# Entering the second attention: loads issued beside the last expert chunks, the norm in two halves, buffers laid out in another order

## The reference, cut to what matters

```python
# L1 ffn, per token: 8 routed experts of width 176 (2 chosen) and a shared one of 352
h1 = jnp.einsum('td,edh->eth', X, W1); h3 = jnp.einsum('td,edh->eth', X, W3)
y = jnp.einsum('eth,ehd->etd', jax.nn.silu(h1) * h3, W2)
out = jnp.einsum('etd,te->td', y, gate_full) + shared
x = x + out
# L2 attention on xn = layernorm(x): 16 query heads, 4 key/value heads, head width 128
q = rms_norm((xn @ wq), q_norm_w); k = rms_norm((xn @ wk), k_norm_w); v = xn @ wv
k_ctx = rms_norm(h_ctx_kv @ wk_ctx, k_norm_w); v_ctx = h_ctx_kv @ wv_ctx
q, k = q * cos + rotate_half(q) * sin, k * cos + rotate_half(k) * sin
probs = softmax(q @ concat([k_ctx, k]).T / sqrt(128) + causal)
x = x + (probs @ concat([v_ctx, v])).reshape(B, L, -1) @ wo
```

## Time and profile before

| | us |
|---|---|
| median of 3 runs | 2813.79 |
| lowest and highest | 2811.82, 2817.29 |
| the profiled execution, its own time | 2814.49 |
| its span | 2812.8 |
| PE busy | 2549.3 (91%) |
| DVE, ACT, POOL busy | 1729.9, 1483.5, 1358.1 |

### The profile page before, as it was taken

The page is one execution under the profiler, slowest core; times in us unless marked ns, Lnnn a source line. Parts: engine busy times, 40 slices in busy tenths (PEclk is TensorE's granted clock), DMA queues, the critical chain, the costliest instruction groups (busy, mean ns, idle before and its releaser), DMA issues. The chain is left out here.

```text
span 2812.8 us, 49623 instructions
## 1 busy us (share of the span) xinstructions
PE 2549.3 (91%) x16226; PEld 1756.5 (62%) x16226; DVE 1729.9 (62%) x3342; ACT 1483.5 (53%) x3294; POOL 1358.1 (48%) x913
## 2 busy tenths in 40 slices
PE   6889998949999999999999999999599699999997
PEld 4577776726777777777777777777355344444443
DVE  4355757547777777777777777777213655454445
ACT  2235444424555665555655555665113567676895
POOL 0025644414666765666756666767101365656400
PEclk9989999978999999999999999999699799999999
DMA  4212222120001000010000100002201000000100
GB/s 158 67 63 85 85 86 73 57 99 13 16 16 44 16 16 2 16 44 16 16 17 1 44 16 17 16 1 120 96 12 58 16 17 15 17 15 17 47 2 16
DMA packets 42454, 108.61 MB, mean 39 GB/s; under 512 B 5044, under 2 KB 26040, under 8 KB 37048
## 3 DMA queue, kind: packets, MB, share of 16 engines
q1 hardware_dynamic: 40424, 102.41, 10.9%
q0 software_dynamic: 768, 2.10, 0.2%
q10 hardware_dynamic: 1008, 0.79, 0.1%
HBM read 99.91 MB, written 4.98 MB: 37 GB/s over the span
## 5 line engine op out<-in xcount | busy, mean ns | idle before, releaser
L1141 POOL TENSOR_TENSOR xn<-xn,l_p 128x512 f32<-128x512 f32 (+1 forms) x400 | 631.4, 1578 | 176.0 <-ACT l_p L1181 155.4
L2120 ACT ACTIVATE l_p<-psum 128x1024 f32<-128x1024 f32 x416 | 394.4, 1022 | 132.6 <-PE psum L2240 132.3
L1266 DVE TENSOR_TENSOR l_plo<-l_p,l_phi 128x512 fp32r<-128x512 f32 (+1 forms) x464 | 398.9, 861 | 94.7 <-ACT l_p L1181 74.5
L1180 ACT ACTIVATE l_phi<-psum 128x512 fp32r<-128x512 f32 (+1 forms) x464 | 279.9, 603 | 272.8 <-PE psum L446 156.8
L1309 DVE TENSOR_REDUCE l_mx<-psum 128x1 f32<-128x512 f32 (+2 forms) x512 | 312.9, 618 | 77.0 <-PE psum L1470 72.8
L2094 POOL TENSOR_TENSOR l_rs<-l_ms,half_power 128x32 f32<-128x32 f32 x45 | 245.2, 5459 | 88.9 <-DVE l_ms L2145 88.9
L1181 ACT ACTIVATE l_p<-psum 128x512 f32<-128x512 f32 (+1 forms) x464 | 281.7, 607 | 0.0
L2240 PE MATMUL psum<-l_qT,l_kT 128*32 128x512 f16 x3328 | 256.4, 384 | 3.3 <-DVE l_qT L2001 2.9
L2250 PE MATMUL psum<-l_p,l_vs 128*32 128x256 f32 x3328 | 254.2, 380 | 0.3 <-ACT l_p L2120 0.3
L1470 PE MATMUL psum<-l_kThi,l_qThi 128*128 128x512 f32 (+2 forms) x512 | 212.4, 441 | 37.7 <-ACT l_kThi L1231 27.0
L1406 PE MATMUL psum<-l_m,l_ones 128*128 128x512 f32 (+1 forms) x464 | 227.3, 490 | 0.0
(11 more groups left out here) (375 smaller groups left out, 5228.4 us busy)
## 6 DMA issues: line engine op xcount, KB each, us to landing
w_stage<-in_L_w_dram SPq DMA_DIRECT2D x76, 384.0 KB, 3.1
l_w<-in_L_w_qkv_dram SPq DMA_DIRECT2D x16, 1024.0 KB, 4.9
l_ct<-in_ctx_tiles_dram SPq DMA_DIRECT2D x52, 128.0 KB, 2.1
c_T<-in_ctx_T_dram SPq DMA_DIRECT2D x4, 1601.0 KB
l_ctx<-in_ctx_T_dram SPq DMA_DIRECT2D x4, 1601.0 KB, 6.8
c_N<-in_ctx_dram SPq DMA_DIRECT2D x4, 1536.0 KB
s_wg<-in_L_gate_dram SPq DMA_DIRECT2D x4, 1024.0 KB, 11.5
s_wu<-in_L_up_dram SPq DMA_DIRECT2D x4, 1024.0 KB, 13.5
```

Source lines behind the costliest of these rows:

```text
L1141: g_.tensor_tensor(l2_acc[k][0:r, :], first[0:r, :], l2_p[c % 3][0:r, :], ALU.add)\
L1180: act.activation(l2_phi[c % 3][0:r, :], src, ACT.Exp).then_inc(l2_e, 1)
L1266: v.tensor_tensor(l2_plo[c % 3][0:r, :], l2_p[c % 3][0:r, :], l2_phi[c % 3][0:r, :].bitcast(F32), ALU.subtract)\
L2120: act.activation(l3_p[ring[c]][:, :], psum[:, (c % 2) * 2 * BANK:(c % 2 + 1) * 2 * BANK], ACT.Exp, scale=float(D3) ** -0.5).then_inc(l3_e, 1)
```

## The change

**The norm of the first half** (tiles 0 to 3) moves beside the last expert block: statistics on DVE and root on POOL at its chunk 5, rows on DVE at chunk 6, four transposes on PE and one copy on ACT at chunk 8 and again at chunk 10, through the bank `AUX`.

**The norm of the second half** (tiles 4 to 7) moves into the opening turn: statistics and root at step 12, rows at step 15, eight transposes and two copies at step 20. Only batches 2 and 3 read it.

**SP** issues `l2_ctx` and the first `l2_w` right behind the last expert weights, then waits for the first half's copies and issues `l2_xb`. After `x_upd` it issues the five small loads, then `l2_wo` on a semaphore of its own (`l2_oland`, for which PE waits before each output product), then the copies to `s_in`.

**POOL** clears the two `l2_m` and `l2_kraw` in place of DVE. ACT and DVE wait for all of POOL's constants (`later_consts` at 5) and five loads before the first copy and the rope products.

**Buffers** of this attention, of the next feed-forward stage (with a pad `s_pad`) and of the last attention are allocated in another order. No wait there is changed by it except the counts shown.

```diff
@@ expert stage @@
+        ATTENTION_NORMS = (NORMS[3][-1] + 1, NORMS[3][-1] + 2)
+        HALF_CP = (2 * len(BLOCKS) + 2, 2 * len(BLOCKS) + 4)
+        ATTENTION_STEP = {"stats": 5, "root": 5, "rows": 6, "turn0": 8, "turn1": 10}
+
+        def attention_rows(v, hf):
+            v.wait_ge(h_rs, ATTENTION_NORMS[hf] + 1)
+            for n in half_tiles(hf):
+                ins = v.tensor_scalar(xn[:, n, :], x[:, n, :], mv[:, n, 0:1], rstd[:, n:n + 1], ALU.subtract, ALU.mult)
+            ins.then_inc(h_xn, 1)
+
+        def attention_turn(pe, hf, c, at):
+            for n in half_tiles(hf):
+                mm = pe.transpose(bank(at, P, (n % HT) * P), xn[:, n, c * P:(c + 1) * P], ident[:, :])
+            mm.then_inc(h_T, 1)
+
+        def attention_copy(act, hf, c, at):
+            act.wait_ge(h_T, 2 * (len(BLOCKS) + hf) + c + 1)
+            act.activation(xT[:, c, half_cols(hf)], bank(at), ACT.Copy).then_inc(h_cp, 1)
...
                     if new is None:
+                        if i == ATTENTION_STEP["root"]:
+                            norm_root(g, ATTENTION_NORMS[0], 0)
                         continue
...
                     if new is None:
+                        for c in range(DC):
+                            if i == ATTENTION_STEP[f"turn{c}"]:
+                                attention_copy(act, 0, c, AUX)
                         continue
...
+                    elif i == ATTENTION_STEP["stats"]:
+                        v.wait_ge(x_upd, OUT_UPD[2])
+                        norm_stats(v, x_rows, 0)
+                    elif i == ATTENTION_STEP["rows"]:
+                        attention_rows(v, 0)
...
             else:
-                pe.wait_ge(x_upd, OUT_UPD[k - 1])
+                pe.wait_ge(h_cp, HALF_CP[0])
...
+                        if i == ATTENTION_STEP["turn0"]:
+                            pe.wait_ge(h_xn, len(BLOCKS) + 1)
+                            pe.wait_ge(x_upd, OUT_UPD[2])
+                            attention_turn(pe, 0, 0, AUX)
+                        if i == ATTENTION_STEP["turn1"]:
+                            pe.wait_ge(h_cp, 2 * len(BLOCKS) + 1)
+                            attention_turn(pe, 0, 1, AUX)
@@ second attention @@
+        SECOND_HALF_AT = (12, 12, 15, 20)
...
         def l2x_sync(sp):
-            sp.wait_ge(x_upd, X_AT[4])
-            rows = t["x"].rearrange("b s d -> (b s) d")
-            sp.dma_start(s_in[0:NTOK, :], rows).then_inc(s_pland, 16)
-            sp.dma_start(s_in[NTOK:TILES2 * P, :], rows[0:TILES2 * P - NTOK, :]).then_inc(s_pland, 16)
-            for dst, name in ((l2_cos, "rope_cos"), (l2_sin, "rope_sin"), (l2_kwc, "L2_kwc"), (l2_wo, "L2_wo")):
-                sp.dma_start(dst[...], t[name]).then_inc(l2_pland, 16)
...
-            sp.wait_ge(xT_cp, ln_l2x["cp_end"])
...
+            for b in range(B):
+                need(sp, l2_proj, b * (KH * NPROJ))
+                sp.dma_start(l2_ctx[:, :, :], t["ctx_T"][b]).then_inc(l2_cland, 16)
+                if b == 0:
+                    sp.dma_start(l2_w[:, :, :], t["L2_w_qkv"][0]).then_inc(l2_wland, 16)
+                sp.wait_ge(h_cp, HALF_CP[b // (B // 2)])
+                sp.dma_start(l2_xb[:, :, :], xT[:, :, b * S:(b + 1) * S]).then_inc(l2_cland, 16)
+                if b == 0:
+                    sp.wait_ge(x_upd, X_AT[4])
+                    for dst, name in ((l2_cos, "rope_cos"), (l2_sin, "rope_sin"), (l2_kwc, "L2_kwc")):
+                        sp.dma_start(dst[...], t[name]).then_inc(l2_pland, 16)
+                    for dst, name in ((l2_qw, "L2_qw"), (l2_kw, "L2_kw")):
+                        sp.dma_start(dst[:, :], t[name].to_broadcast([P, HD])).then_inc(l2_pland, 16)
+                    sp.dma_start(l2_wo[:, :, :], t["L2_wo"]).then_inc(l2_oland, 16)
...
+        def l2_clear(g):
+            g.wait_ge(x_upd, X_AT[4])
+            for s in range(2):
+                pool_steps.then(g, g.memset(l2_m[s][:, :, :].bitcast(F32), 0.0))
+            g.memset(l2_kraw[0][:, :, :], 0.0).then_inc(later_consts, 1)
...
+                    if g is None and c == SECOND_HALF_AT[1]:
+                        norm_root(g_, ATTENTION_NORMS[1], 1)
...
         def l2x_scalar(act):
-            norm_scalar(act, ln_l2x)
             act.preload_act_table(ACT.Exp)
-            act.wait_ge(l2_pland, 16 * 6)
+            act.wait_ge(l2_pland, 16 * 5)
+            act.wait_ge(later_consts, 5)
...
+                    if g is None and c == SECOND_HALF_AT[3]:
+                        for d in range(DC):
+                            attention_copy(act, 1, d, 3 + d)
...
         def l2x_vector(v):
             v.wait_ge(x_upd, X_AT[4])
-            dve_steps.then(v, v.memset(l2_kraw[0][:, :, :], 0.0))
...
-                dve_steps.then(v, v.memset(l2_m[s][:, :, :].bitcast(F32), 0.0))
-            v.wait_ge(l2_pland, 16 * 6)
+            v.wait_ge(later_consts, 5)
+            v.wait_ge(l2_pland, 16 * 5)
...
-            norm_vector(v, ln_l2x, x)
...
+                    if g is None and c == SECOND_HALF_AT[0]:
+                        norm_stats(v, x_rows, 1)
+                    if g is None and c == SECOND_HALF_AT[2]:
+                        attention_rows(v, 1)
...
         def l2x_tensor(pe):
-            norm_tensor(pe, ln_l2x)
...
                 if half == 0:
+                    pe.wait_ge(l2_oland, 16)
                     pe.wait_ge(l2_o, g * TB + (k + 1))
...
+                    if g is None and c == SECOND_HALF_AT[3]:
+                        pe.wait_ge(h_xn, len(BLOCKS) + 2)
+                        for d in range(DC):
+                            attention_turn(pe, 1, d, 3 + d)
...
+        sb("s_pad", [P, S_PAD], F32, top)
```

More of the change, by code:

```diff
@@ L39 @@
 TILES2 = NT + E2 - 1
+S_PAD = 2112
 QH, KH, HD = 16, 4, 128
@@ L981, in program @@
         TURNS = B * KH
-        l2_ctx = sb("l2_ctx", [P, DC, M], F32, l2)
-        l2_w = sb("l2_w", [P, DC, 4 * HD + REP * HD], F32, l2)
-        l2_xb = sb("l2_xb", [P, DC, S], F32, l2)
-        l2_kraw = [sb(f"l2_kraw{n}", [P, 4, HD], F32, l2) for n in range(2)]
-        l2_kn = [sb(f"l2_kn{n}", [P, 4, HD], F32, l2) for n in range(2)]
-        l2_ra = sb("l2_ra", [P, TB, HD], F32, l2)
-        l2_rb = sb("l2_rb", [P, TB, HD], F32, l2)
-        l2_q = sb("l2_q", [P, TB, REP, HD], F32, l2)
-        l2_qa = sb("l2_qa", [P, TB, REP, HD], F32, l2)
-        l2_qb = sb("l2_qb", [P, TB, REP, HD], F32, l2)
         def l2_slot(s):
@@ L1018, in program @@
         l2_ones = sb("l2_ones", [P, P], F32R, l2)
+        l2_wo = sb("l2_wo", [P, QH, D], F32, l2)
+        l2_ra = sb("l2_ra", [P, TB, HD], F32, l2)
+        l2_rb = sb("l2_rb", [P, TB, HD], F32, l2)
+        l2_q = sb("l2_q", [P, TB, REP, HD], F32, l2)
+        l2_qa = sb("l2_qa", [P, TB, REP, HD], F32, l2)
+        l2_qb = sb("l2_qb", [P, TB, REP, HD], F32, l2)
+        l2_xb = sb("l2_xb", [P, DC, S], F32, l2)
+        l2_ctx = sb("l2_ctx", [P, DC, M], F32, l2)
+        l2_w = sb("l2_w", [P, DC, 4 * HD + REP * HD], F32, l2)
+        l2_kraw = [sb(f"l2_kraw{n}", [P, 4, HD], F32, l2) for n in range(2)]
+        l2_kn = [sb(f"l2_kn{n}", [P, 4, HD], F32, l2) for n in range(2)]
+        l2_vhi, l2_vlo, l2_kThi, l2_kTlo, l2_qThi, l2_qTlo, l2_m = zip(l2_slot(0), slot1)
         l2.close()
+        l2_oland = sem("l2_oland")
         (l2_cland, l2_wland, l2_pland, l2_proj, l2_qc, l2_kvc, l2_vl, l2_ksqd, l2_kmsd, l2_krsd, l2_qmsd, l2_qrsd,
@@ new lines, in l2x_sync @@
+            for b in range(B):
[12 more added lines that the diff above has]
+                    sp.dma_start(l2_wo[:, :, :], t["L2_wo"]).then_inc(l2_oland, 16)
+                    rows = t["x"].rearrange("b s d -> (b s) d")
+                    sp.dma_start(s_in[0:NTOK, :], rows).then_inc(s_pland, 16)
+                    sp.dma_start(s_in[NTOK:TILES2 * P, :], rows[0:TILES2 * P - NTOK, :]).then_inc(s_pland, 16)
+                    with sp.Fori(1, KH) as h:
+                        head_weights(b, h)
+                else:
+                    with sp.Fori(0, KH) as h:
+                        head_weights(b, h)
@@ L1596, in program @@
         s_eidf, s_eid = sb("s_eidf", [1, TILES2], F32, top), sb("s_eid", [1, TILES2], I32, top)
+        sb("s_pad", [P, S_PAD], F32, top)
+        s_wg = sb("s_wg", [P, E2, DC, F2], F32, top)
+        s_wu = sb("s_wu", [P, E2, DC, F2], F32, top)
+        s_xT = sb("s_xT", [P, DC, TILES2 * P], F32, top)
         top.close()
@@ L2309, in program @@
         f3.close()
-        kept.close()
         f3_wland = sems("f3_wland", 3)
```

65 lines of the change are left out of this document (26 added, 39 removed).

## The result

| us | before | changed |
|---|---|---|
| median, first comparison (4 runs each) | 2813.79 | 2773.89 |
| lowest and highest | 2811.82, 2817.29 | 2771.79, 2776.16 |
| profiled execution, its own time | 2814.49 | 2772.86 |
| span, granted clock over it | 2812.8, 0.959 | 2771.1, 0.967 |
| mean of all runs of this study | 2811.6 (96 runs) | 2775.9 (16 runs) |

Three more comparisons of the same two kernels gave 0.9878 (0.9864 to 0.9892), 0.9868 (0.9853 to 0.9883) and 0.9873 (0.9858 to 0.9888). Over all runs the change saves 35.7 us. So half of the miss was in the first two samples, as the experiments show.

A forecast was written before the change was run, and what follows sets the result against it. PE was taken to bound the kernel, with one deep idle hole before the second attention's first projection. Terms -35.1 + 0.9 + 2.1 + 0.5 = -31.6 us gave 2782.9, adjusted to 2782.2; range for 8 in 10: 2777 to 2793.

The forecast's parts named there:

- ACT's first copy, -35.1: Entry of the second attention: ACT's first copy moves from 603.64 to 568.5, the small loads ending last; -35.1 us.
- I take 2.9: Entry of the second attention: the last small load, `l_kw`, issued at 565.5, takes 2.9 us to land.
- Last block, +0.9: Last expert block: two groups of four transposes added on PE each stretch a chunk; +0.9 us in all.
- Opening turn, +2.1: Opening turn: second half's norm adds 0.6 at step 12, 0.25 at step 15, 1.2 at step 20; +2.1 us.
- The wait for `l2_oland`, +0.5: Steady turns: one more wait ahead of 32 output products, at most 1.9 us, taken as +0.5 us.
- The new places of the buffers change no wait and no size, and I take 0: Steady turns: the buffers' new addresses were taken to cost or save nothing, 0 us.
- what is saved in the hole should reach the end of the program undiminished: Time saved between last expert chunk and second attention's first projection was to reach the end in full, PE having almost no idle time.
- The clock stays low after the entry: Rival: the clock falls after the entry and the opening turn runs low, +10 us less 2 to 3; 2790; chance 0.14.
- The clock does better: Rival: the low stretch of 16.5 us in the opening turn shrinks, 3 to 4 us less; 2779; chance 0.11.
- Another wait: Rival: at the entry, small loads or POOL's chain come late, ACT starting at up to 574.9; 2788.6; chance 0.07.
- loads not ahead: Rival: SP reaches `l2_ctx` late and the projection waits; 10 us beyond the 22 us slack give 2792; chance 0.03.
- Slower by the layout: Rival: new buffer places slow the 464 steady key chunks; 0.1 us per chunk would give 2828.6; chance 0.03.

The follow-up runs named there:

- small loads first: Changed kernel with the five small loads issued with the weights into own memory and POOL clearing `l2_kraw` first; mean 2772.3 us, 0.9858 and 0.9855 of the kernel before.
- `c2_loads_late`: Changed kernel with only the early loads undone, so context and weights wait for the complete x; mean 2782.3 us.

## Why the prediction was wrong, point by point

**The forecast, in the terms of the repeated traces.** Means over three traces before and four after:

| us | before | changed | difference | forecast |
|---|---|---|---|---|
| x complete | 562.8 | 564.0 | +1.2 | +0.9 |
| hole | 41.3 | 6.7 | -34.6 | -35.1 |
| opening | 47.0 | 48.5 | +1.5 | +2.1 |
| rest | 2160.4 | 2155.3 | -5.1 | +0.5 |
| sum | 2811.5 | 2774.5 | -37.0 | -31.6 |

- *ACT's first copy, -35.1.* Right in mechanism (the small loads end last), 0.5 too much, and that close by some luck: the forecast hole is 5.6 us (568.5 - 562.87) and the measured one 6.4 to 7.3, but the hole before was 0.5 us longer on average than in the one trace I had. The step that was mis-sized is "I take 2.9": 5.1 in the first trace and 4.1 to 4.3 in the others, because `l2_wo` and x are issued right behind `l_kw`; with these held back it was 3.1. POOL's clears took 0.96 ns per element, next to the 0.86 of the earlier trace rows, and DVE's clears of the same buffer had taken 0.91 us for 1024 (0.89 ns). The half rate that the section "Performance versus the Vector engine" of "GPSIMD Engine Reference" in the Trainium skill gives is measured there on a two-input addition; these clears, which read nothing, don't show it.
- *"at the low clock they had before".* The first projection ran at 2.4 GHz (3.60 us, not 5.28). It changed nothing, since the small loads ended last.
- *Last block, +0.9.* Two chunks grew by some 0.47 us each. The mean of +1.2 has scatter in it.
- *Opening turn, +2.1.* 1.5 by the repeated traces, 0.8 to 1.6 by leaving the pieces out.
- *The wait for `l2_oland`, +0.5.* Nothing that shows.
- *"The new places of the buffers change no wait and no size, and I take 0".* This term failed: waits and sizes stayed, yet PE's products became shorter, `l_phi` by `l_vlo` from 396 to 393 ns, and the loop by some 2 us. The argument that "no length in this trace goes with an address" could not be drawn from a single trace, in which the addresses never change.
- *The failed step* in the main is "what is saved in the hole should reach the end of the program undiminished", with "the steady turns keep their length": what was saved did reach the end, but the rest behind it was not the same length. The rest was taken to be fixed by the program at the 2162.9 us of the only trace there was. It wanders between 2157.3 and 2162.9 in that kernel. My own sign, equal turns more than 2 us apart, came true inside single traces (batches of 337.0 and 339.6 us in the second trace of the kernel before), and the two batches of the kernel before (339.32 and 337.64 us), which I had not set side by side, would have shown it.

Of the 8.3 us by which the first median missed, 2.2 are the base (2813.8 in four runs, 2811.6 in 96) and 2.0 the first four runs of the changed kernel (2773.9, 2775.9 in 16). The remaining 4.1 lie, by the traces, behind the first score matmul. Of these 1.3 go with the comparison's own offset, which unaltered code shows too (35.7 us saved by all runs, 34.4 by those in the same place), and some 2 are the buffers' order, by the traces. That leaves under 1 us, below what these runs resolve. The rests alone would not tell it: all six traces with the old instructions (two with the new order of buffers, one shifted) have a mean of 2158.8 us, all twelve with the new ones 2156.0, and in both sets single traces differ by 7 us.

**The rivals.** *The clock stays low after the entry*: it did fall, twice or three times in the opening turn. Windows of PE over the opening in three traces, before, changed (third) and small loads first:
```profile
603.64:649.83 46.19, 34.46 (x123) 0.86 0.06 23
```
```profile
568.47:617.17 48.70, 36.25 (x128) 0.78 0.21 84
```
```profile
565.25:612.65 47.40, 33.75 (x131) 0.93 0.24 96
```
From 0.93 to 0.78 the turn is 1.3 us longer, but these are two programs. Within one, 0.78 instead of 0.82 (the third trace of the changed kernel against its first, some 4 us more at 1.2 GHz) went with 0.8 us, 48.70 against 47.91. I had priced a turn that stays low for its 13 steps at 10 us; only 17 to 21 us of it were low, against 12.5 to 17 before, so that price was not put to the test. In that turn PE waits for DVE and ACT, and a low stretch is mostly absorbed. In the top stage, where PE is busy for three quarters of the time, a granted 0.79 instead of 0.82 cost 2.7 us. *The clock does better*: closing PE's wait for ACT (5.96 us, in which the clock fell at 568.8) kept 1.00 from 562 to 599.9 in the first trace of the small-loads version. That is what "The HAM clock gate" in the Trainium skill's "TensorE: Matmul & The Clock Gate" has as its rule (activity lifts the clock, an idle gap loses it); this trace agrees, but the opening turn is only about 1 us shorter in it. *Another wait, loads not ahead*: neither came. *Slower by the layout*: the layout does change PE's products, but to the better. Had the loads come late, it would have cost 6.4 us, by `c2_loads_late`.

The range was the second fault: 2777 left 5.2 us below the forecast for everything, while single runs of either kernel scatter by 3 us (standard deviation), so that the difference of two samples of four is off by some 2 us from chance alone.

## What to carry to other kernels

Before forecasting to a few us, look at how equal parts of one trace differ (here batches of 336.8 and 338.4 us): that spread, times the number of parts, belongs in the range, and the base is a mean and not one execution. Behind a chain that is cut, the next thing is often the last small load; issue small loads ahead of what they wait for in their own memory, and keep large transfers out of their queue until they land. Measure the unaltered kernel as if it were a change, before a difference of 0.1% is believed. And where the times can't tell, compare equal parts of several traces, here two turns without their idle time and without a dip: they repeat to 0.05 us and found an effect of 0.28 us that 22 runs against 22 did not.

## What the runs showed of the hardware

- At the loop's end, where PE is idle for 1.67 to 2.22 us, the clock fell to 1.2 GHz for 3.4 us behind 22 of 108 such idle times, and at the same place in one execution of a program and not in another. One such dip costs some 1.9 us (170.1 to 170.7 us for two turns against 168.2 to 169.1).
- The price of a low clock depends on the stage: 0.8 us for some 4 us more at 1.2 GHz in the opening turn, where PE waits for others (48.70 against 47.91 us); 1.9 us for 3.4 us in the steady turns; 2.7 us for 6.8 us (0.79 instead of 0.82 over 120 us) in the top stage.
- The same 464 products took 395 or 396 ns each in one order of the buffers in SBUF and 393 or 394 in another, with the same instructions; all buffers shifted by 64 bytes in one order changed nothing (396).
- The last of five small loads landed 3.1 us after its issue with nothing behind it, and 5.1, 4.3, 4.1 and 4.2 us after it with a 2 MB transfer issued 0.5 us behind.
- POOL cleared 1024 elements a partition in 0.98 us, DVE in 0.91.
